# Distances from f32r high and low parts, and a schedule with one query or key projection per slot

## The chip, the cores and the metric

The kernel runs on one core of one Trainium2 chip. The metric is the device time of one execution in microseconds (us), from the first to the last instruction and what lies around them. Matrix products run on TensorE (PE in the profile, its weight loads PEld), elementwise work on VectorE (DVE), ScalarE (ACT) and GpSimd (POOL); the transfers of this kernel are issued by the SyncE queue (SP).

## The reference, cut to what matters

Four layers follow each other on x of shape (8, 512, 128): a distance attention, a mixture of experts, a linear attention, a block with token selection. The change touches only the first:

```python
def _cdist(Q, K):
    q2 = jnp.sum(Q * Q, axis=-1)
    k2 = jnp.sum(K * K, axis=-1)
    qk = jnp.einsum('hbtd,hbsd->hbts', Q, K)
    d2 = q2[..., :, None] + k2[..., None, :] - 2.0 * qk
    return jnp.sqrt(jnp.maximum(d2, 0.0))
P = X @ W_in + b_in                       # 16 heads, each 64 of Q, K, V, G
Q, K, V, G = jnp.split(P, splits, axis=-1)
W = jnp.power(EPS + _cdist(Q, K), -P_POW) # EPS 1e-4, P_POW 2
W = W / (EPS + jnp.sum(W, axis=-1, keepdims=True))
A = jnp.einsum('hbts,hbse->hbte', W, V)
H = G * A
return H @ W_out + b_out                  # heads side by side again
```

## The kernel before, in words

`build_attention` computes the first layer, `build_rest` the other three; the second begins when the first has ended. Each engine has its own instruction list, in a fixed order written out by hand, and the engines meet in semaphores.

The attention goes over 8 batches of 512 tokens. A batch has 16 heads, taken four at a time (a quad): 32 periods `j`, four to a batch (`q = j % 4`). Two heads (a pair, `r` = 0 or 1) lie one above the other in the 128 partitions, 64 rows each, so a product over 64 rows is issued once for each half `v`. Each period has four slots `k`. In slot `k` of period `j`, in this order, TensorE does (lines 401 to 427):

- `distances(j, k)`: two chunks `i` of 128 keys against 512 queries for the two heads, into the four banks of `sc`. Per chunk and half, two f32r products of the matrix `quarter` (0.25) with the high and the low part of the squared queries (L356), then one f32 product key by query (L361; the query is stored times -2). A wait on `s_d2` lets a slot begin once VectorE has emptied `sc`.
- projections for period `j + 1`: slot 0 Q0 and K0, slot 1 Q1 and K1, slot 2 G0, slot 3 G1. Each is three f32r products of split operands (`product`, L57) into a bank of `pj`.
- slot 0 `sums(j-2)` (column sums of the weights that POOL has added, L382), slot 1 `output(j-3)` (L390), slot 2 `weighted_values(j-1, 0)` (L374) and `key_norms(j+1)` (16 records of L342), slot 3 `weighted_values(j-1, 1)`; once per batch eight `values` products (four in slot 3 of q = 0, four in slot 1 of q = 1) and transposes in slot 2 of q = 2.

`pj` has three banks, used in rotation by everything but the distances and `weighted_values`. The list `bank_uses` numbers the uses; use number n waits until VectorE has emptied use n-3 (`bank`, line 306):

```python
n = use[name]
if n >= 3:
    pe.wait_ge(s_pj_free, n - 2)
return n % 3
```

VectorE goes through the same slots in the same order: four operations that add the key norms, cut at 0 and write `w` (L495), one operation for each projection (L472, L474, L478), then the gate times the values (L502), the sums (L507), the reciprocals (L511) and so on; in slot 0 of q = 2 `norm_apply` (L624, L627) for the next batch. ScalarE takes root, logarithm and exponential of `w` (L584, L588, L598). POOL has per period: `normalize(j-3)` (L287), `squares(j+1, 0)` and `squares(j+1, 1)` (L260, L264, L268, L270 each), then `add_chunks(j-1, u)` for u = 0 to 3, three adds each (L278, L281). `normalize` waits for the broadcast reciprocals, which go by way of four transfers of the SP queue from the sums of slot 0 and the reciprocals of slot 2 of the period before. `query` and `key` have three places each, so POOL may read them late.

Of the kernel before, what the change touches and what calls it, by code (L numbers as in the profile page):

```python
# [20 lines left out]
P = 128  # L21
# [39 lines left out]
def build_attention(nc, a, x1, dsum, drec):  # L61
# [3 lines left out]
    with ExitStack() as ctx:  # L65
# [15 lines left out]
        xn = sb("xn", [P, NC, D])  # L81
# [11 lines left out]
        quarter = sb("quarter", [P, P], F32R)  # L93
        ones = sb("ones", [P, 32])

        query = sb("query", [P, 3, T])
        key = sb("key", [P, 3, T])
        sqq = sb("sqq", [P, T])
        sqk = sb("sqk", [P, 2, T])
        sqs = [sb("sq_h", [P, 3, T], F32R), sb("sq_l", [P, 3, T], F32R)]  # L100
        k2 = sb("k2", [P, 2, 2, NC, 2])
        gT = sb("gT", [P, PAIRS, T])
# [30 lines left out]
        s_pj_free = sem("s_pj_free")  # L133
        s_sq = sem("s_sq")
# [24 lines left out]
        def bank_uses(j, k):  # L159
            names = []  # L160
            b, q = divmod(j, QUADS)
            if j + 1 < NQ:
                names += [("p", j + 1, i) for i in (((Q0, K0), (Q1, K1), (G0,), (G1,))[k])]
            if k == 0 and 0 <= j - 2 < NQ:
                names.append(("sum", j - 2))
            if k == 1 and q == 1 and b < B:
                names += [("v", b, n) for n in range(4, 8)]
            if k == 1 and 0 <= j - 3 < NQ:
                names.append(("out", j - 3))
            if k == 2 and j + 1 < NQ:  # L170
                names.append(("k2", j + 1))
# [26 lines left out]
        def _(sp):  # L198
# [19 lines left out]
            sp.wait_ge(s_xn, NC)  # L218
# [20 lines left out]
            for j in range(NQ):  # L239
# [5 lines left out]
                if q == 1 and b + 2 < B:  # L245
                    sp.wait_ge(s_xn, NC * (b + 2))
                    load_x(xa, b + 2, s_xa)
# [3 lines left out]
        def _(pool):  # L251
            nc.gpsimd.memset(ones[:, :], 1.0).then_inc(s_ones, 1)
            nc.gpsimd.memset(quarter[:, :].bitcast(F32), 0.25).then_inc(s_ones, 1)

            def squares(j, r):
# [4 lines left out]
                nc.gpsimd.tensor_tensor(sqq[:, :], query[:, g % 3, :], query[:, g % 3, :], ALU.mult).then_inc(s_sq, 1)  # L260
                pool.wait_ge(s_pj_free, use["p", j, 3 * r + 1] + 1)
                if j >= 1:
                    pool.wait_ge(s_pj, use["k2", j - 1] + 1)
                nc.gpsimd.tensor_tensor(sqk[:, r, :], key[:, g % 3, :], key[:, g % 3, :], ALU.mult).then_inc(s_sq, 1)  # L264
# [18 lines left out]
            def normalize(j):  # L283
# [4 lines left out]
                                        gT[:, 2 * q:2 * q + 2, :], ALU.mult).then_inc(s_hT, 1)  # L288

            for j in PERIODS:  # L290
                if 0 <= j - 3 < NQ:
                    normalize(j - 3)
                if j + 1 < NQ:
                    squares(j + 1, 0)
                    squares(j + 1, 1)
# [9 lines left out]
        def _(pe):  # L305
# [6 lines left out]
            def turn(b):  # L312
                pe.wait_ge(s_xn, NC * (b + 1))
                for h in range(2):
                    n = bank(("turn", b, h))
                    for c in range(2 * h, 2 * h + 2):
                        m = nc.tensor.transpose(pj[:, n, c % 2 * P:(c % 2 + 1) * P], xn[:, c, :], ident[:, :])
# [83 lines left out]
            def step(j, k):  # L401
# [3 lines left out]
                if j + 1 < NQ:  # L405
                    for i in ((Q0, K0), (Q1, K1), (G0,), (G1,))[k]:
                        projection(j + 1, i)
                if k == 0 and 0 <= j - 2 < NQ:
                    sums(j - 2)
# [921 lines left out]
```

## Time and profile before

| | before |
|---|---|
| runs, us | 1567.01, 1563.69, 1568.65 (median 1567.01) |
| profiled execution, us | 1569.49 |
| its span, us | 1567.7 |
| PE busy | 1466.7 (94%) |
| DVE busy | 977.1 (62%) |
| ACT busy | 1039.0 (66%) |
| POOL busy | 817.1 (52%) |
| granted TensorE clock, mean | 0.967 |
| attention, us from the span's start | 0 to about 1031 |

A busy time is the sum of an engine's instructions; matmul ends are modelled, so spacing of starts tells more than a duration. A granted clock of 1 is 2.4 GHz, of 0.5 it is 1.2 GHz. POOL has all its work in the attention.

### The profile page before, as it was taken

Reading aid. Unit: us, or ns where it says so; the run is one execution under the profiler, and the core shown is the slowest. Engines: PE = TensorE matmul, PEld = TensorE weight load, DVE = VectorE, ACT = ScalarE, POOL = GpSimd, SP = SyncE. Lnnn points to the kernel's source line nnn. Section 1 sums busy time; section 2 is a strip of 40 time slices with the busy share of each in tenths; the row PEclk is TensorE's granted clock in tenths of the full one; section 3 lists DMA queues with packets and bytes.
Section 4 is the critical chain, followed back from the end, with each engine's and each line's share of the span. In section 5 each row is a group of like instructions: output and inputs, shape, how many; then the busy total and the mean of one; then the engine's idle time right before and its main releaser. Section 6 shows DMA issues by size and latency. Waiting matters only on the chain. (4 is left out here: it accounts for less than half of the span.)

```text
span 1567.7 us, 18478 instructions
## 1 busy us (share of the span) xinstructions
PE 1466.7 (94%) x6704; PEld 811.4 (52%) x6704; DVE 977.1 (62%) x2082; ACT 1039.0 (66%) x834; POOL 817.1 (52%) x681
## 2 busy tenths in 40 slices
PE   6999999999999999999999999559999999999984
PEld 4544544554544544545545444135666666666653
DVE  4766676666666766776676665134375675665664
ACT  1789779869968977977977878424454554554531
POOL 5678878878879879879879878500000000000000
PEclk9999999999999999999999999769999999999995
DMA  3000010011001002001101101161110110110100
GB/s 106 1 15 22 15 42 22 14 36 28 15 15 48 15 15 49 15 15 38 25 15 28 28 15 40 30 196 59 54 61 1 61 61 1 62 55 7 61 5 10
DMA packets 45851, 54.96 MB, mean 35 GB/s; under 512 B 13824, under 2 KB 32640, under 8 KB 44608
## 3 DMA queue, kind: packets, MB, share of 16 engines
q1 hardware_dynamic: 45760, 53.77, 11.4%
q8 instruction: 54, 0.88, 0.2%
q14 instruction: 37, 0.30, 0.1%
HBM read 48.91 MB, written 4.85 MB: 34 GB/s over the span
## 5 line engine op out<-in xcount | busy, mean ns | idle before, releaser
L495 DVE TENSOR_SCALAR w<-sc,k 128x512 f32<-128x512 f32 x512 | 348.9, 743 | 148.2 <-PE sc L361 121.3
L584 ACT ACTIVATE w<-w 128x2048 f32<-128x2048 f32 x128 | 237.5, 1904 | 193.6 <-DVE w L495 193.2
L281 POOL TENSOR_TENSOR wsum<-wsum,w 128x512 f32<-128x512 f32 x256 | 327.1, 1278 | 20.1
L846 ACT ACTIVATE hr<-z,b 128x512 f32<-128x512 f32 x256 | 175.6, 686 | 226.4 <-PE z L57 226.3
L993 PE MATMUL y<-hr,w 128*128 128x512 f32 x512 | 261.4, 593 | 2.4 <-DVE yT L1199 2.4
L361 PE MATMUL sc<-query,key 64*128 64x512 f32 x1024 | 243.7, 594 | 0.0
L374 PE MATMUL av<-w,vt 128*64 128x512 f32 x1024 | 236.1, 603 | 6.7 <-ACT w L598 5.8
L588 ACT ACTIVATE w<-w 128x2048 f32<-128x2048 f32 x128 | 240.3, 1901 | 0.4
L598 ACT ACTIVATE w<-w 128x2048 f32<-128x2048 f32 x128 | 239.6, 1896 | 0.0
L57 PE MATMUL z<-xs_h,w_h 128*128 128x512 f32 x256 | 202.1, 789 | 0.1
L278 POOL TENSOR_TENSOR wsum<-w 128x512 f32<-128x512 f32 x128 | 163.5, 1277 | 8.8 <-ACT w L598 8.8
L260 POOL TENSOR_TENSOR sqq<-query 128x512 f32<-128x512 f32 x64 | 66.6, 1041 | 154.4 <-DVE query L472 154.2
L374 PEld LDWEIGHTS av<-w,vt 128*64 128x64 f32 x1024 | 68.6, 138 | 143.8 <-issue 136.0
L361 PEld LDWEIGHTS sc<-query,key 64*128 64x128 f32 x1024 | 99.7, 188 | 72.4 <-issue 61.4
L356 PE MATMUL sc<-sq_h,quarter 64*128 64x512 f32 x512 | 115.8, 447 | 12.6 <-DVE w L495 12.6
L502 DVE TENSOR_TENSOR gT<-av,gT 128x512 f32<-128x512 f32 x64 | 44.2, 691 | 131.3 <-PE av L374 131.3
L356 PE MATMUL sc<-sq_l,quarter 64*128 64x512 f32 x512 | 102.2, 393 | 0.0
L57 PE MATMUL z<-xs_l,w_h 128*128 128x512 f32 x256 | 101.4, 396 | 0.0
L993 PEld LDWEIGHTS y<-hr,w 128*128 128x128 f32 x512 | 90.7, 189 | 19.8 <-DVE yT L1199 2.8
L57 PE MATMUL z<-xs_h,w_l 128*128 128x512 f32 x256 | 100.9, 394 | 0.0
L1199 DVE SCALAR_TENSOR_TENSOR ye<-y,b,rb 128x512 f32<-128x512 f32 x56 | 41.9, 749 | 90.5 <-PE y L993 90.3
L356 PEld LDWEIGHTS sc<-sq_h,quarter 64*128 64x128 f32 x512 | 48.9, 185 | 92.0 <-issue 79.8
(154 smaller groups left out, 2166.6 us busy)
## 6 DMA issues: line engine op xcount, KB each, us to landing
hT<-head_recips SPq DMA_DIRECT2D x64, 256.0 KB, 4.0
rb<-routing SPq DMA_DIRECT2D x8, 2048.0 KB, 7.1
w<-in_W SPq DMA_DIRECT2D x16, 256.0 KB, 6.2
xa<-in_X SPq DMA_DIRECT2D x8, 256.0 KB, 4.5
xc<-in_X SPq DMA_DIRECT2D x8, 256.0 KB, 2.8
x<-xc SPq DMA_DIRECT2D x8, 256.0 KB, 4.1
out<-prod SPq DMA_DIRECT2D x8, 256.0 KB, 2.3
x<-x SPq DMA_DIRECT2D x1, 1792.0 KB, 10.2
```

The lines of the kernel that those rows point to most:

```text
L57: m = nc.tensor.matmul(out, lhsT[u], rhs[v], start=start and i == 0, stop=stop and i == 2)
L278: nc.gpsimd.tensor_tensor(wsum[:, u, :], w[:, j % 2, u, 0, :], w[:, j % 2, u, 1, :], ALU.add).then_inc(s_added, 1)
L281: nc.gpsimd.tensor_tensor(wsum[:, u, :], wsum[:, u, :], w[:, j % 2, u, c, :], ALU.add).then_inc(s_added, 1)
L356: nc.tensor.matmul(sc[:, i, v, :], quarter[halves[v], :], sqs[part][halves[v], g % 3, :], start=(part == 0), stop=False)
L361: m = nc.tensor.matmul(sc[:, i, v, :], key[halves[v], g % 3, c * P:(c + 1) * P], query[halves[v], g % 3, :], start=False, stop=True)
L374: m = nc.tensor.matmul(av[64 * v:64 * v + 64, :], vt[:, c, (2 * g + v) * E0:(2 * g + v + 1) * E0], w[:, j % 2, 2 * r + v, c, :], start=(c ...
L495: nc.vector.tensor_scalar(w[:, s, 2 * r + v, c, :], sc[:, i, v, :], k2[:, s, r, c, v:v + 1], 0.0, ALU.add, ALU.max).then_inc(s_d2, 1)
L584: nc.scalar.activation(w[:, slot, u, :, :], w[:, slot, u, :, :], ACT.Sqrt).then_inc(s_sqrt, 1)
L588: nc.scalar.activation(w[:, slot, u, :, :], w[:, slot, u, :, :], ACT.Ln, bias=ATT_EPS).then_inc(s_ln, 1)
L598: nc.scalar.activation(w[:, slot, u, :, :], w[:, slot, u, :, :], ACT.Exp, scale=-2.0).then_inc(s_w, 1)
L846: nc.scalar.activation(hr[:, n % 8, :], z[:, n % 2, :], ACT.Relu, bias=b1[:, n % NU:n % NU + 1]).then_inc(S["hr"], 1)
L993: m = nc.tensor.matmul(y[:, g % 2, :], w2[:, k, :], hr[:, n % 8, :], start=(i == 0), stop=(i == NF - 1))
```

## The change

The f32 product of key and query is replaced by three f32r products of high and low parts: key high by query high, key high by query low, key low by query high, each in the two row halves (per slot 12 instructions of one pass, where there were 4 of two passes). For that VectorE makes three operations of each query and key projection: the whole value (for POOL's squares), the high part in f32r, and, after a wait on the new semaphore `s_high`, the difference as the low part; the bank is handed back by the third. `query` and `key` have one place now, so the write of the whole value waits on `s_sq` until POOL has squared the one before. Signs and factors change (`quarter` 0.25 becomes `half` -0.5, the query is no longer times -2, VectorE subtracts and takes the minimum, the root has scale -2.0), with the same number of operations.

The order changes on TensorE and VectorE alike: slots 0 to 3 have Q0, K0, Q1, K1 of period `j + 1`; the gates G0 and G1 of period `j - 1` come in slots 0 and 1 (one period before they are used up, `gT` has two places in place of eight pairs). The key norms of the second pair are made in slot 1 of the next period, those of the first in slot 2, 8 records each. In slot 1 `output` stands ahead of `values`. POOL squares the second pair at the start of its own period, after `normalize`, then the first pair of the next. The normalized input is written over `xa` (`xn` is gone), and the SP queue loads the next `xa` after the transposes in place of after the normalization. The `step` functions of both engines (lines 401 and 527) follow `bank_uses` below.

```diff
@@ -90,16 +89,18 @@
         nsel = sb("nsel", [P, 2, P])
-        quarter = sb("quarter", [P, P], F32R)
+        half = sb("half", [P, P], F32R)
         ones = sb("ones", [P, 32])
...
-        query = sb("query", [P, 3, T])
-        key = sb("key", [P, 3, T])
+        query = sb("query", [P, T])
+        key = sb("key", [P, T])
+        queries = [sb("query_h", [P, 3, T], F32R), sb("query_l", [P, 3, T], F32R)]
+        keys = [sb("key_h", [P, 3, T], F32R), sb("key_l", [P, 3, T], F32R)]
         sqq = sb("sqq", [P, T])
-        sqk = sb("sqk", [P, 2, T])
+        sqk = sb("sqk", [P, T])
         sqs = [sb("sq_h", [P, 3, T], F32R), sb("sq_l", [P, 3, T], F32R)]
         k2 = sb("k2", [P, 2, 2, NC, 2])
-        gT = sb("gT", [P, PAIRS, T])
+        gT = sb("gT", [P, 2, 2, T])
         hT = sb("hT", [P, 2, 2, T])
...
@@ -160,15 +162,19 @@
             if j + 1 < NQ:
-                names += [("p", j + 1, i) for i in (((Q0, K0), (Q1, K1), (G0,), (G1,))[k])]
+                names.append(("p", j + 1, (Q0, K0, Q1, K1)[k]))
+            if k < 2 and 0 <= j - 1 < NQ:
+                names.append(("p", j - 1, (G0, G1)[k]))
             if k == 0 and 0 <= j - 2 < NQ:
                 names.append(("sum", j - 2))
+            if k == 1 and 0 <= j < NQ:
+                names.append(("k2", j, 1))
+            if k == 1 and 0 <= j - 3 < NQ:
+                names.append(("out", j - 3))
             if k == 1 and q == 1 and b < B:
                 names += [("v", b, n) for n in range(4, 8)]
-            if k == 1 and 0 <= j - 3 < NQ:
-                names.append(("out", j - 3))
             if k == 2 and j + 1 < NQ:
-                names.append(("k2", j + 1))
+                names.append(("k2", j + 1, 0))
             if k == 2 and q == 2 and b >= 1:
...
@@ -243,25 +249,25 @@
                 if q == 1 and b + 2 < B:
-                    sp.wait_ge(s_xn, NC * (b + 2))
+                    sp.wait_ge(s_pj, use["turn", b + 1, 1] + 1)
                     load_x(xa, b + 2, s_xa)
...
             nc.gpsimd.memset(ones[:, :], 1.0).then_inc(s_ones, 1)
-            nc.gpsimd.memset(quarter[:, :].bitcast(F32), 0.25).then_inc(s_ones, 1)
+            nc.gpsimd.memset(half[:, :].bitcast(F32), -0.5).then_inc(s_ones, 1)
...
                     pool.wait_ge(s_sq, 4 * g)
-                nc.gpsimd.tensor_tensor(sqq[:, :], query[:, g % 3, :], query[:, g % 3, :], ALU.mult).then_inc(s_sq, 1)
+                nc.gpsimd.tensor_tensor(sqq[:, :], query[:, :], query[:, :], ALU.mult).then_inc(s_sq, 1)
                 pool.wait_ge(s_pj_free, use["p", j, 3 * r + 1] + 1)
-                if j >= 1:
-                    pool.wait_ge(s_pj, use["k2", j - 1] + 1)
-                nc.gpsimd.tensor_tensor(sqk[:, r, :], key[:, g % 3, :], key[:, g % 3, :], ALU.mult).then_inc(s_sq, 1)
+                if g >= 1:
+                    pool.wait_ge(s_pj, use["k2", *divmod(g - 1, 2)] + 1)
+                nc.gpsimd.tensor_tensor(sqk[:, :], key[:, :], key[:, :], ALU.mult).then_inc(s_sq, 1)
                 pool.wait_ge(s_sq, 4 * g + 1)
...
@@ -285,14 +291,15 @@
                 nc.gpsimd.tensor_tensor(hT[:, j % 2, :, :], hT[:, j % 2, :, :],
-                                        gT[:, 2 * q:2 * q + 2, :], ALU.mult).then_inc(s_hT, 1)
+                                        gT[:, j % 2, :, :], ALU.mult).then_inc(s_hT, 1)
...
                     normalize(j - 3)
+                if 0 <= j < NQ:
+                    squares(j, 1)
                 if j + 1 < NQ:
                     squares(j + 1, 0)
-                    squares(j + 1, 1)
                 if j == -1:
...
@@ -333,14 +340,12 @@
-            def key_norms(j):
-                n = bank(("k2", j))
-                pe.wait_ge(s_sq, 8 * j + 6)
-                for r in range(2):
-                    for c in range(NC):
-                        i = 2 * (NC * r + c)
-                        m = nc.tensor.matmul(pj[:, n, i:i + 2], sqk[:, r, c * P:(c + 1) * P], nsel[:, 0, 0:64:32],
-                                             start=(i == 0), stop=True, skip_group_check=True)
+            def key_norms(j, r):
+                n = bank(("k2", j, r))
+                pe.wait_ge(s_sq, 8 * j + 4 * r + 2)
+                for c in range(NC):
+                    m = nc.tensor.matmul(pj[:, n, 2 * c:2 * c + 2], sqk[:, c * P:(c + 1) * P], nsel[:, 0, 0:64:32],
+                                         start=(c == 0), stop=True, skip_group_check=True)
                 m.then_inc(s_pj, 1)
...
@@ -351,15 +356,15 @@
                 for i in range(2):
+                    c = 2 * k % NC + i
                     for part in range(2):
                         for v in range(2):
-                            nc.tensor.matmul(sc[:, i, v, :], quarter[halves[v], :], sqs[part][halves[v], g % 3, :],
+                            nc.tensor.matmul(sc[:, i, v, :], half[halves[v], :], sqs[part][halves[v], g % 3, :],
                                              start=(part == 0), stop=False)
-                for i in range(2):
-                    c = 2 * k % NC + i
-                    for v in range(2):
-                        m = nc.tensor.matmul(sc[:, i, v, :], key[halves[v], g % 3, c * P:(c + 1) * P],
-                                             query[halves[v], g % 3, :], start=False, stop=True)
+                    for part, (x, y) in enumerate(((0, 0), (0, 1), (1, 0))):
+                        for v in range(2):
+                            m = nc.tensor.matmul(sc[:, i, v, :], keys[x][halves[v], g % 3, c * P:(c + 1) * P],
+                                                 queries[y][halves[v], g % 3, :], start=False, stop=(part == 2))
                     m.then_inc(s_sc, 1)
...
@@ -464,28 +470,33 @@
             def projection(j, i):
-                q = j % QUADS
                 r, part = divmod(i, 3)
-                s = (2 * j + r) % 3
-                source, bias = pj[:, bank(("p", j, i)), :], bqkg[:, 2 * q + r, part:part + 1]
-                if part == 0:
-                    nc.vector.tensor_scalar(query[:, s, :], source, bias, -2.0, ALU.add, ALU.mult).then_inc(s_pj_free, 1)
-                elif part == 1:
-                    nc.vector.tensor_scalar(key[:, s, :], source, bias, None, ALU.add).then_inc(s_pj_free, 1)
-                else:
-                    if j >= QUADS:
-                        dve.wait_ge(s_hT, j - QUADS + 1)
-                    nc.vector.tensor_scalar(gT[:, 2 * q + r, :], source, bias, None, ALU.add).then_inc(s_pj_free, 1)
-
-            def key_norms(j):
-                nc.vector.tensor_copy(k2[:, j % 2, :, :, :].rearrange("p r c v -> p (r c v)"),
-                                      pj[:, bank(("k2", j)), 0:4 * NC]).then_inc(s_pj_free, 1)
+                g = 2 * j + r
+                n = bank(("p", j, i))
+                source, bias = pj[:, n, :], bqkg[:, 2 * (j % QUADS) + r, part:part + 1]
+                if part == 2:
+                    if j >= 2:
+                        dve.wait_ge(s_hT, j - 1)
+                    nc.vector.tensor_scalar(gT[:, j % 2, r, :], source, bias, None, ALU.add).then_inc(s_pj_free, 1)
+                    return
+                whole, (high, low) = (query, queries) if part == 0 else (key, keys)
+                if g >= 1:
+                    dve.wait_ge(s_sq, 4 * (g - 1) + part + 1)
+                nc.vector.tensor_scalar(whole[:, :], source, bias, None, ALU.add)
+                nc.vector.tensor_scalar(high[:, g % 3, :], source, bias, None, ALU.add).then_inc(s_high, 1)
+                dve.wait_ge(s_high, 2 * g + part + 1)
+                nc.vector.scalar_tensor_tensor(low[:, g % 3, :], source, bias, high[:, g % 3, :].bitcast(F32),
+                                               ALU.add, ALU.subtract).then_inc(s_pj_free, 1)
+
+            def key_norms(j, r):
+                nc.vector.tensor_scalar(k2[:, j % 2, r, :, :].rearrange("p c v -> p (c v)"),
+                                        pj[:, bank(("k2", j, r)), 0:2 * NC], 0.5, None, ALU.mult).then_inc(s_pj_free, 1)
...
                 s, r = j % 2, k // 2
-                if k == 0:
-                    dve.wait_ge(s_pj_free, use["k2", j] + 1)
+                if k % 2 == 0:
+                    dve.wait_ge(s_pj_free, use["k2", j, r] + 1)
                 if j >= 2:
...
@@ -493,13 +504,12 @@
                         nc.vector.tensor_scalar(w[:, s, 2 * r + v, c, :], sc[:, i, v, :], k2[:, s, r, c, v:v + 1], 0.0,
-                                                ALU.add, ALU.max).then_inc(s_d2, 1)
+                                                ALU.subtract, ALU.min).then_inc(s_d2, 1)
...
             def weighted_values(j, r):
-                g = 2 * (j % QUADS) + r
                 dve.wait_ge(s_av, 2 * j + r + 1)
                 dve.wait_ge(s_pj_free, use["p", j, 3 * r + 2] + 1)
-                nc.vector.tensor_tensor(gT[:, g, :], av[:, :], gT[:, g, :], ALU.mult).then_inc(s_gated, 1)
+                nc.vector.tensor_tensor(gT[:, j % 2, r, :], av[:, :], gT[:, j % 2, r, :], ALU.mult).then_inc(s_gated, 1)
...
@@ -581,7 +592,7 @@
                     act.wait_ge(s_d2, 16 * j + 2 * (4 * r + 3) + v + 1)
-                    nc.scalar.activation(w[:, slot, u, :, :], w[:, slot, u, :, :], ACT.Sqrt).then_inc(s_sqrt, 1)
+                    nc.scalar.activation(w[:, slot, u, :, :], w[:, slot, u, :, :], ACT.Sqrt, scale=-2.0).then_inc(s_sqrt, 1)
...
                     act.wait_ge(s_sqrt, j * 4 + u + 1)
```

## Rows read from the trace of the kernel before

**Rows 1.** Page: busy us of each engine, share of the span, instructions.

```profile
PE 1466.7 (94%) x6704; PEld 811.4 (52%) x6704; DVE 977.1 (62%) x2082; ACT 1039.0 (66%) x834; POOL 817.1 (52%) x681
```

**Rows 2.** Timeline, PE, one period: start us, length, engine, line, out<-in, count, [idle].

```profile
503.44 0.50 PE L356 MATMUL sc<-sq_h,quarter 64*128 64x512 f32 x2
...
508.87 0.50 PE L356 MATMUL sc<-sq_h,quarter 64*128 64x512 f32 x2
...
515.01 0.50 PE L356 MATMUL sc<-sq_h,quarter 64*128 64x512 f32 x2
...
522.32 1.95 PE L342 MATMUL pj<-nsel,sqk 128*128 128x2 f32 x16
...
524.19 0.50 PE L356 MATMUL sc<-sq_h,quarter 64*128 64x512 f32 x2
...
525.23 1.88 PE L361 MATMUL sc<-query,key 64*128 64x512 f32 x8
...
527.04 0.50 PE L57 MATMUL pj<-xh,wqkg_h 128*128 128x512 f32 x1
...
527.61 0.40 PE L57 MATMUL pj<-xl,wqkg_h 128*128 128x512 f32 x1
...
527.93 3.65 PE L374 MATMUL av<-w,vt 128*64 128x512 f32 x16
...
531.52 0.50 PE L57 MATMUL pj<-wv_h,xh 128*128 128x512 f32 x1
```

**Rows 3.** Timeline, DVE: the copy of the key norms, four periods apart.

```profile
403.37 0.17 DVE L481 COPY k<-pj 128x16 f32<-128x16 f32 x1 [1.17 <-PE pj L342]
...
524.30 0.17 DVE L481 COPY k<-pj 128x16 f32<-128x16 f32 x1 [1.17 <-PE pj L342]
```

**Rows 4.** Timeline, DVE, slot 0 and the start of slot 1 of one period.

```profile
505.66 2.73 DVE L495 TENSOR_SCALAR w<-sc,k 128x512 f32<-128x512 f32 x4 [1.42 <-PE sc L361]
...
508.30 0.74 DVE L472 TENSOR_SCALAR query<-pj,bqkg 128x512 f32<-128x512 f32 x1
...
509.62 0.68 DVE L507 TENSOR_SCALAR srow<-pj 128x512 f32<-128x512 f32 x1
```

**Rows 5.** Timeline, DVE: a cast and the subtraction that waits for it (experts' weights).

```profile
1037.04 0.43 DVE L1186 CAST w_h<-w 128x512 fp32r<-128x512 f32 x1
...
1037.50 0.69 DVE L1188 TENSOR_TENSOR w_l<-w,w_h 128x512 fp32r<-128x512 f32 x1
```

**Rows 6.** Page, costliest groups: out<-in xcount | busy us, mean ns | idle before, releaser.

```profile
L1199 DVE SCALAR_TENSOR_TENSOR ye<-y,b,rb 128x512 f32<-128x512 f32 x56 | 41.9, 749 | 90.5 <-PE y L993 90.3
```

**Rows 7.** Timeline, PE: a use of pj that waited for its bank.

```profile
424.59 0.50 PE L57 MATMUL pj<-wv_h,xh 128*128 128x512 f32 x1 [0.45 <-DVE query L472]
```

**Rows 8.** Timeline, POOL: squares, the first of twelve adds, and the next normalize.

```profile
579.44 1.04 POOL L260 TENSOR_TENSOR sqq<-query 128x512 f32<-128x512 f32 x1 [3.71 <-DVE query L472]
580.44 1.04 POOL L264 TENSOR_TENSOR sqk<-key 128x512 f32<-128x512 f32 x1
...
583.36 1.28 POOL L278 TENSOR_TENSOR wsum<-w 128x512 f32<-128x512 f32 x1
...
599.14 2.41 POOL L287 TENSOR_TENSOR hT<-hT,gT 128x1024 f32<-128x1024 f32 x1
```

**Rows 9.** Timeline, DVE: `norm_apply` with POOL idle, and with POOL at work.

```profile
5.42 1.11 DVE L627 TENSOR_SCALAR xn<-xa,mv,rstd 128x128 f32<-128x128 f32 x4
...
573.06 3.01 DVE L627 TENSOR_SCALAR xn<-xa,mv,rstd 128x128 f32<-128x128 f32 x4
```

**Rows 10.** Who waited for whom, 60 to 1130 us: total us, times, longest.

```profile
POOL hT L287 <- DMA hT<-head_recips: 16.2, 9, 11.2
```

**Rows 11.** Timeline, PE: work after idle stretches, at full and at half clock.

```profile
21.70 3.54 PE L342 MATMUL pj<-nsel,sqk 128*128 128x2 f32 x16 [2.82 <-POOL sqk L264]
...
92.17 0.50 PE L356 MATMUL sc<-sq_h,quarter 64*128 64x512 f32 x2 [2.83 <-DVE w L495]
...
1008.98 3.75 PE L390 MATMUL pj<-hT,wout 128*128 128x512 f32 x4 [2.47 <-POOL hT L287]
```

More of the change, by code:

```diff
@@ L80, in build_attention @@
         holder = sb("holder", [P, 1])
-        xn = sb("xn", [P, NC, D])
         xs = [sb("xh", [P, 2, T], F32R), sb("xl", [P, 2, T], F32R)]
@@ L133, in build_attention @@
         s_pj_free = sem("s_pj_free")
+        s_high = sem("s_high")
         s_sq = sem("s_sq")
@@ L217, in _ @@
             load_x(xc, 0, s_xc)
-            sp.wait_ge(s_xn, NC)
+            sp.wait_ge(s_pj, use["turn", 0, 1] + 1)
             load_x(xa, 1, s_xa)
@@ L316, in turn @@
                     for c in range(2 * h, 2 * h + 2):
-                        m = nc.tensor.transpose(pj[:, n, c % 2 * P:(c % 2 + 1) * P], xn[:, c, :], ident[:, :])
+                        m = nc.tensor.transpose(pj[:, n, c % 2 * P:(c % 2 + 1) * P], xa[:, c, :], ident[:, :])
                     m.then_inc(s_pj, 1)
@@ L405, in step @@
                 if j + 1 < NQ:
-                    for i in ((Q0, K0), (Q1, K1), (G0,), (G1,))[k]:
-                        projection(j + 1, i)
+                    projection(j + 1, (Q0, K0, Q1, K1)[k])
+                if k < 2 and 0 <= j - 1 < NQ:
+                    projection(j - 1, (G0, G1)[k])
                 if k == 0 and 0 <= j - 2 < NQ:
                     sums(j - 2)
+                if k == 1 and 0 <= j < NQ:
+                    key_norms(j, 1)
+                if k == 1 and 0 <= j - 3 < NQ:
+                    output(j - 3)
                 if k == 1 and q == 1 and b < B:
@@ L412, in step @@
                         values(b, n)
-                if k == 1 and 0 <= j - 3 < NQ:
-                    output(j - 3)
-                if k == 2 and 0 <= j - 1 < NQ:
-                    weighted_values(j - 1, 0)
+                if k >= 2 and 0 <= j - 1 < NQ:
+                    weighted_values(j - 1, k - 2)
                 if k == 2 and j + 1 < NQ:
-                    key_norms(j + 1)
+                    key_norms(j + 1, 0)
                 if k == 2 and q == 2 and b >= 1:
@@ L422, in step @@
                     turn(b + 1)
-                if k == 3 and 0 <= j - 1 < NQ:
-                    weighted_values(j - 1, 1)
                 if k == 3 and q == 0 and b < B:
@@ L449, in norm_apply @@
             def norm_apply(b):
-                layernorm_apply(nc, dve, xa, 0, xn, mv, std[:, :], rstd[:, :], b, s_std, s_rstd, s_xn)
+                layernorm_apply(nc, dve, xa, 0, xa, mv, std[:, :], rstd[:, :], b, s_std, s_rstd, s_xn)
             def turned(b):
@@ L531, in step @@
                 if j + 1 < NQ:
-                    for i in ((Q0, K0), (Q1, K1), (G0,), (G1,))[k]:
-                        projection(j + 1, i)
+                    projection(j + 1, (Q0, K0, Q1, K1)[k])
+                if k < 2 and 0 <= j - 1 < NQ:
+                    projection(j - 1, (G0, G1)[k])
                 if k == 0 and 0 <= j - 2 < NQ:
@@ L537, in step @@
                     norm_apply(b + 1)
+                if k == 1 and 0 <= j < NQ:
+                    key_norms(j, 1)
+                if k == 1 and 0 <= j - 3 < NQ:
+                    output(j - 3)
                 if k == 1 and q == 1 and b < B:
@@ L542, in step @@
                         norm_stats(b + 1)
-                if k == 1 and 0 <= j - 3 < NQ:
-                    output(j - 3)
-                if k == 2 and 0 <= j - 1 < NQ:
-                    weighted_values(j - 1, 0)
+                if k >= 2 and 0 <= j - 1 < NQ:
+                    weighted_values(j - 1, k - 2)
                 if k == 2 and j + 1 < NQ:
-                    key_norms(j + 1)
+                    key_norms(j + 1, 0)
                 if k == 2 and q == 2 and b >= 1:
@@ L554, in step @@
                     turned(b + 1)
-                if k == 3 and 0 <= j - 1 < NQ:
-                    weighted_values(j - 1, 1)
                 if k == 3 and q == 0 and b < B:
```

## Prediction, made before the changed kernel was run

> **What bounds the kernel now.** I read the busy shares first: PE is busy 94% of the span, no other engine over 66% [rows 1]. Next the timeline of TensorE over one period in the steady stretch. Its starts follow each other without a hole: distances of slot 0 at 503.44, of slot 1 at 508.87, of slot 2 at 515.01, of slot 3 at 524.19, and the last work of the plain period ends where the values begin, at 531.52 [rows 2]. So the slots last 5.43, 6.14, 9.18 and 7.33 us, a plain period 28.08, and TensorE's own work sets it. Four periods (a batch, with eight value products and a normalization) last 524.30 - 403.37 = 120.93 us [rows 3], 30.2 on the average.
>
> **What TensorE saves.** In slot 3 the four f32r pairs of the squares take 525.23 - 524.19 = 1.04 us (0.34 to the second, then 0.23 each; the halves of a pair run beside each other). The key-query products are eight records, 527.04 - 525.23 = 1.81 us. Then three products of 0.23 and a transition: 527.93 - 527.04 = 0.89 [rows 2]. After the change the slot has 2 x 2 + 2 x 3 = 10 f32r pairs and the three products in one run: 0.34 + 11 x 0.23 + 0.32 = 3.20 us to the weighted values, where there were 3.74. That is 0.54 a slot; the new pairs have the form of the squares' pairs (64 rows, 64x512), so I take their spacing. The key norms move 8 of their 16 records from slot 2 to slot 1: (524.19 - 522.32) / 2 = 0.93 us [rows 2]. The projections are two, two, one, one per slot as before. New slots: 4.89, 6.53, 7.71, 6.79; sum 25.92, a saving of 2.16 a period and 69 us in 32, if TensorE stays the bound.
>
> **What VectorE gets.** Spacing in rows: four distance operations 508.30 - 505.66 = 2.64, one projection (509.62 - 508.30) / 2 = 0.66 [rows 4]. A projection of a query or key becomes three. The whole value costs 0.66. The high part ends before the low part may start: 0.74 and a hop; a cast and the subtraction that waits for it start 0.46 apart with 0.43 busy [rows 5], so 0.78. The low part is a three-operand operation, 0.75 by the experts' own [rows 6] (0.69 as a plain subtraction [rows 5]), 0.67 to the next start. Sum 2.11, or 2.19 until the bank is free, in place of 0.66 or 0.74. Four a period: 5.8 us more. VectorE stays under 90%, which would be hidden; what counts is where it lies.
>
> **The bank.** With the new order the uses of `pj` in slot 1 are K0, G1, key norms, output; `output` is three uses behind K0 and waits for its low part. (Before, it came three behind the sums.) The rows show such a wait once a batch: a value product three uses behind Q1 waited 0.45 us for the query operation [rows 7]. Count from the start of TensorE's slot 0. The first chunk of distances is ready after five pairs, 1.5 us. VectorE then runs without a hole: distances 2.64, Q0 2.11, G0 0.66, sums 0.60, distances of slot 1 2.64, K0 2.19: bank free at 12.35. TensorE would be at `output` at 4.89 + 0.34 + 15 x 0.23 + 0.1 + 0.93 = 9.7. It waits 2.7 us there. From there output 1.85 (its share of slot 1, with the hop), slot 2 7.71, slot 3 6.79: the plain period is **28.7**, 0.6 longer than before, although TensorE works 2.2 less.
>
> **POOL's loop.** `query` has one place, so VectorE's Q0 of the next period waits until POOL has squared Q1 of the one before, and POOL does that only after twelve adds and `normalize`. Who is queued behind: on VectorE everything of slot 0 after the distances, then the distances of slot 1 and K0; on POOL the adds wait behind the squares of K0. That closes a ring. POOL, from K0 handed over: hop 0.08, square of the key to the first add 583.36 - 580.44 = 2.92, the adds 599.14 - 583.36 = 15.78, `normalize` 2.35, square of Q1 1.04 [rows 8], hop 0.05: 22.2. VectorE, from the start of Q0 to K0 handed over: 2.11 + 0.66 + 0.60 + 2.64 + 2.19 = 8.2. Ring: **30.4 us**. It is longer than the bank's 28.7, so it sets plain periods. In the trace of before POOL never stood in a ring: it waited 3.71 for the query here [rows 8].
>
> **Sum over a batch.** q = 0: four value products in slot 3 (12 x 0.23 + 0.2 = 3.0) lie in the bank's path, not in POOL's: 28.7 + 3.0 = 31.7. q = 1: four value products after output, the same 31.7. q = 2: `norm_apply` lies between sums and the distances of slot 1, in both paths. It takes 3.01 beside POOL's work and 1.11 where POOL is idle [rows 9]; at its new place POOL has only the end of one square left and then waits for K0, so I take 1.6 (bounds 1.3 and 3.2): 32.0. q = 3: 30.4. Sum 125.8, against 120.93: +4.9 a batch, +34 us over periods 3 to 31. The first three periods lack `output` and part of POOL's list: -2. The last has no projections to make and only saves: -2. The start-up gains and loses (POOL's splitting of weights now stands ahead of the second squares; VectorE's operations are longer): taken at 0, bounds -4 and +4. Layers two to four (from 1031 us) are untouched. The order of the SP queue costs nothing: the transposes it now waits for lie in q = 2, and the queue gets to that wait only after the reciprocals of q = 3. The DMA of the reciprocals is a third path to `normalize`; it kept POOL waiting 16.2 us in all, 11.2 of it at the end of the attention, so about 5 in the rest [rows 10], and POOL now comes later. Total +30 to +31. Against the profiled execution's 1569.5 that is 1600; its own time lies 2.5 over the median, so against the median 1598.
>
> **The rivals.**
> The clock falls in the new wait (chance 0.20). The wait at `output` is 2.7 us in q = 0 and 1 up to some 4 in q = 2, and the 2-column key norms lie ahead of it. In the rows one idle stretch of 2.82 was followed by key norms in 3.54 us (1.95 elsewhere [rows 2]), so at 1.2 GHz; another of 2.83 was followed by work at 2.4 GHz; after 2.47 with little work ahead `output` took 3.75 for 1.88 [rows 11]. If it falls in most periods, about 5 us of work at half rate lose 2.6 each, and TensorE's path is the longer one: 31.3, 34.3 twice, 33.9, in a batch 133.8, +12.9, +90 in all less 4: 1653.
> The Trainium skill, page "TensorE: Matmul & The Clock Gate", section "Why this matters for your kernels", warns that idle gaps between bursts of matmuls bring the array back to half rate; by that rule this rival would be the rule in q = 2 and a matter of luck elsewhere.
> Only the bank (0.13): POOL's ring turns out shorter than 28.7, by shorter adds or an earlier start. Then 31.7, 31.7, 31.3, 28.7: +2.5 a batch, 1567 + 17 - 4 = 1580.
> TensorE stays the bound (0.12), the other side: the wait for K0 is hidden, because VectorE catches up or the f32r operations write faster than an f32 one (a cast of the same size takes 0.43 [rows 5]). With 2.2 saved a period and nothing given back: 1567 - 69 = 1498. It decides as soon as K0's bank is free 9.7 us into the period; VectorE's work ahead of that would have to shrink by 2.7 of 12.3 us, and POOL's ring by as much again, so it is not likely.
> The halves of the new pairs don't run beside each other (0.05): 6 x 0.23 = 1.4 more per slot, 3.5 in the bank's path: 28.7 becomes 32.2, a batch 137.4, 1567 + 115 - 4 = 1678. Against it: the squares' pairs do run so [rows 2].
>
> **How the numbers follow.** Forecast (bank and POOL's ring together, clock up) 0.50, time 1598. With a slow `norm_apply` it would be 11 higher (1.6 a batch of seven); a ring 0.5 us off moves two periods of four, 7 us; a clock that falls now and then adds 10 to 25. The range leaves out the two outer cases (0.12 and 0.05) and takes in the others: 1575 to 1658. This kernel's runs can tell about 0.3% (5 us). Faster: 0.12 and a rest of the start-up bounds, 0.13. Same: 0.04, the low tail of the bank case. Slower: 0.83.
>
> **What would show it.** Right: on TensorE f32r pairs 0.23 apart through the whole slot; idle time before `output` (L390), released by VectorE's key operation; idle time of VectorE before the query's first operation in slot 0, released by POOL's square; a batch of about 126 us, with plain periods of 30.4; PE's busy time 60 to 70 us lower and its share under 90%; POOL almost without a wait. A granted clock well under 1 between 100 and 950 us would show the clock's case. Wrong: a period under 28 us, `output` without a wait, or f32r operations of VectorE under 0.6 us.

## The result

| | before | after |
|---|---|---|
| median of the runs, us | 1566.6 | 1652.2 (1649.8 to 1653.9) |
| ratio | | 1.0547, 95% interval 1.0523 to 1.0571 |
| profiled execution's span, us | 1567.7 | 1648.9 |
| attention ends at, us from the start | 1031 | 1114 |

The change costs 86 us. Layers two to four are untouched: of the span's 81 us, 82 lie ahead of the first instruction of `build_rest` (1031.4 before, 1113.5 after), so all of it is in the attention.

The page of the changed kernel, the lines that answer to [rows 1]; the third is the group of `output` (line 390 before, 395 now; columns as in [rows 6]):

```profile
PE 1477.6 (90%) x7216; PEld 883.9 (54%) x7216; DVE 1146.0 (70%) x2370; ACT 1039.1 (63%) x834; POOL 819.9 (50%) x681
PEclk9999999999999998999999999977999999999995
...
L395 PE MATMUL pj<-hT,wout 128*128 128x512 f32 x128 | 103.2, 952 | 91.2 <-DVE key_l L488 77.3
```

`output` now has 77.3 us of idle time ahead of it, ended by VectorE's low part of the key, and its records last 952 ns in the mean, where 592 is their mean in the kernel before between 60 and 960 us. TensorE has less work and is busy longer (1477.6 us for 1466.7): part of the work runs at half rate.

Slot 0 and slot 1 of one period (q = 2) of the changed kernel, TensorE and VectorE, and POOL where it waits:

```profile
609.19 2.42 POOL L293 TENSOR_TENSOR hT<-hT,gT 128x1024 f32<-128x1024 f32 x1 [4.00 <-DMA hT<-head_recips]
...
611.82 1.07 PE L387 MATMUL pj<-wsum,ones 128*32 128x512 f32 x8
612.71 0.75 DVE L485 TENSOR_SCALAR query<-pj,bqkg 128x512 f32<-128x512 f32 x1 [0.71 <-POOL sqq L266]
612.81 0.50 PE L362 MATMUL sc<-sq_h,half 64*128 64x512 f32 x2
...
616.28 1.28 DVE L638 TENSOR_SCALAR xa<-xa,mv,rstd 128x128 f32<-128x128 f32 x4
...
616.83 0.95 PE L347 MATMUL pj<-nsel,sqk 128*128 128x2 f32 x8
617.49 2.71 DVE L506 TENSOR_SCALAR w<-sc,k 128x512 f32<-128x512 f32 x4
620.12 0.73 DVE L485 TENSOR_SCALAR key<-pj,bqkg 128x512 f32<-128x512 f32 x1
620.78 0.73 DVE L486 TENSOR_SCALAR key_h<-pj,bqkg 128x512 fp32r<-128x512 f32 x1
621.55 0.75 DVE L488 SCALAR_TENSOR_TENSOR key_l<-pj,bqkg,key_h 128x512 fp32r<-128x512 f32 x1
622.35 3.78 PE L395 MATMUL pj<-hT,wout 128*128 128x512 f32 x4 [4.58 <-DVE key_l L488]
622.38 1.04 POOL L270 TENSOR_TENSOR sqk<-key 128x512 f32<-128x512 f32 x1 [5.67 <-DVE key_l L488]
626.07 0.79 PE L362 MATMUL sc<-sq_h,half 64*128 64x512 f32 x2
```

`output` of the kernel before, at full clock:

```profile
513.20 1.88 PE L390 MATMUL pj<-hT,wout 128*128 128x512 f32 x4
```

In the changed kernel TensorE has done its list of slot 1 up to `output` at 617.8, VectorE comes to K0 at 620.12 and hands its bank back at 622.3, and `output` starts 0.05 us later, at half clock (3.78 us for 1.88). The granted clock is 1.00 from 590.0 to 617.8 us, 0.50 from 622.3 to 627.0 and 0.99 from there to 640.0. The normalization takes 1.28 where it took 3.01 [rows 9]. The reciprocals come once a period, in slot 2 (VectorE, changed kernel):

```profile
533.25 0.24 DVE L521 RECIPROCAL srec<-ssum 128x16 f32<-128x16 f32 x1
...
564.15 0.24 DVE L521 RECIPROCAL srec<-ssum 128x16 f32<-128x16 f32 x1
...
600.88 0.24 DVE L521 RECIPROCAL srec<-ssum 128x16 f32<-128x16 f32 x1
...
635.78 0.24 DVE L521 RECIPROCAL srec<-ssum 128x16 f32<-128x16 f32 x1
...
666.55 0.24 DVE L521 RECIPROCAL srec<-ssum 128x16 f32<-128x16 f32 x1
```

A batch is 666.55 - 533.25 = 133.3 us, where it was 120.9 [rows 3] and the forecast's sum was 125.8; the period up to 564.15 takes 30.9. Who waited for whom in the attention of the changed kernel (total us, times, longest):

```profile
PE pj L395 <- DVE key_l L488: 77.3, 28, 4.6
...
POOL hT L293 <- DMA hT<-head_recips: 43.9, 20, 10.8
...
DVE query L485 <- POOL sqq L266: 8.3, 5, 4.2
```

The wait for K0's bank is there in all 28 full periods, 2.8 us in the mean. VectorE waited for POOL's square five times in all: the ring that the forecast took as the longer path is not what sets most periods of this kernel.

### The profile page after: what moved, and what is told of

The parts are those of the page before. It is cut to its first block and busy times, and to the rows that moved or that the text cites. A ratio compares the mean times of both kernels' runs of the same rounds, so it can differ in the third digit from the quotient of the medians.

```text
span 1648.9 us, 19955 instructions
## 1 busy us (share of the span) xinstructions
PE 1477.6 (90%) x7216; PEld 883.9 (54%) x7216; DVE 1146.0 (70%) x2370; ACT 1039.1 (63%) x834; POOL 819.9 (50%) x681
## 5 line engine op out<-in xcount | busy, mean ns | idle before, releaser
L506 DVE TENSOR_SCALAR w<-sc,k 128x512 f32<-128x512 f32 x512 | 348.4, 742 | 80.4 <-PE sc L366 80.4
L395 PE MATMUL pj<-hT,wout 128*128 128x512 f32 x128 | 103.2, 952 | 91.2 <-DVE key_l L488 77.3
L270 POOL TENSOR_TENSOR sqk<-key 128x512 f32<-128x512 f32 x64 | 66.7, 1042 | 158.7 <-DVE key_l L488 155.7
L362 PE MATMUL sc<-sq_h,half 64*128 64x512 f32 x512 | 121.0, 468 | 4.0 <-DVE w L506 4.0
L362 PE MATMUL sc<-sq_l,half 64*128 64x512 f32 x512 | 105.7, 408 | 0.0
L366 PE MATMUL sc<-query_h,key_h 64*128 64x512 f32 x512 | 104.9, 403 | 0.0
L366 PE MATMUL sc<-query_l,key_h 64*128 64x512 f32 x512 | 104.5, 401 | 0.0
L366 PE MATMUL sc<-query_h,key_l 64*128 64x512 f32 x512 | 104.0, 399 | 0.0
L362 PEld LDWEIGHTS sc<-sq_h,half 64*128 64x128 f32 x512 | 51.3, 195 | 93.4 <-issue 41.7
```

What stands on the lines that cost most here:

```text
L362: nc.tensor.matmul(sc[:, i, v, :], half[halves[v], :], sqs[part][halves[v], g % 3, :], start=(part == 0), stop=False)
L366: m = nc.tensor.matmul(sc[:, i, v, :], keys[x][halves[v], g % 3, c * P:(c + 1) * P], queries[y][halves[v], g % 3, :], start=False, stop=(p ...
L506: nc.vector.tensor_scalar(w[:, s, 2 * r + v, c, :], sc[:, i, v, :], k2[:, s, r, c, v:v + 1], 0.0, ALU.subtract, ALU.min).then_inc(s_d2, 1)
```

## The experiments

Theory A, that of the forecast: K0's bank and POOL's ring. Theory B, its first rival: the bank and the clock that falls in the wait. Rivals to both: the wait alone, TensorE's work, the order of the change as such. Each kernel was compared with the kernel before run on the same chip (1567.5 to 1569.6 in these).

### TensorE's part alone

In the kernel before, with `query` and `key` as f32r tiles; it leaves out the low parts and VectorE's operations for them, and all three products read the same two tiles:

```diff
                 for i in range(2):
+                    c = 2 * k % NC + i
...
-                for i in range(2):
-                    c = 2 * k % NC + i
-                    for v in range(2):
-                        m = nc.tensor.matmul(sc[:, i, v, :], key[halves[v], g % 3, c * P:(c + 1) * P],
-                                             query[halves[v], g % 3, :], start=False, stop=True)
+                    for part in range(3):
+                        for v in range(2):
+                            m = nc.tensor.matmul(sc[:, i, v, :], key[halves[v], g % 3, c * P:(c + 1) * P],
+                                                 query[halves[v], g % 3, :], start=False, stop=(part == 2))
```

> The kernel before, schedule and all, with query and key written once, as f32r, and the f32 product of key and query replaced by three f32r products of these same tiles (the low parts and VectorE's operations for them are left out). It measures what TensorE alone saves. By the spacing in the changed kernel's trace a slot takes 3.43 us to the weighted values where it took 3.74: 0.31 x 128 = 40 us, 1527. By the forecast's 0.54 a slot: 69 us, 1498.

Measured: 1529.0, ratio 0.9748 (0.9730 to 0.9766), 39.4 us faster: 0.31 a slot. The forecast's 0.54 is wrong, and one slot shows by what (TensorE, this kernel):

```profile
526.90 0.50 PE L357 MATMUL sc<-sq_h,quarter 64*128 64x512 f32 x2
...
528.63 0.88 PE L361 MATMUL sc<-query,key 64*128 64x512 f32 x6
529.43 0.50 PE L57 MATMUL pj<-xh,wqkg_h 128*128 128x512 f32 x1
...
530.33 1.94 PE L374 MATMUL av<-w,vt 128*64 128x512 f32 x8
```

The pairs go at 0.23 behind the first step of 0.34, but from the last of them (528.63 + 2 x 0.23 = 529.09) to the first product over all 128 rows it is 0.34, and 0.34 again to the second (at 529.77). I had run pairs and products into one row at 0.23. The slot takes 3.43 us, not 3.20.

### One operation of VectorE in place of three

In the changed kernel, leaving out the whole value and the low part (POOL and the three products then read the f32r part):

```diff
...
-                nc.vector.tensor_scalar(whole[:, :], source, bias, None, ALU.add)
-                nc.vector.tensor_scalar(high[:, g % 3, :], source, bias, None, ALU.add).then_inc(s_high, 1)
-                dve.wait_ge(s_high, 2 * g + part + 1)
-                nc.vector.scalar_tensor_tensor(low[:, g % 3, :], source, bias, high[:, g % 3, :].bitcast(F32),
-                                               ALU.add, ALU.subtract).then_inc(s_pj_free, 1)
+                nc.vector.tensor_scalar(high[:, g % 3, :], source, bias, None, ALU.add).then_inc(s_pj_free, 1)
```

> The changed kernel, schedule and all, with one operation of VectorE for each query and key projection (the f32r part alone; the whole value and the low part are left out, POOL squares the f32r part, the three products read it three times). TensorE's work and order, the banks and POOL's list are those of the changed kernel. Theory: K0's bank is free 2.9 us earlier, 9.5 us into the period, before TensorE comes to output; no wait, no fall of the clock, 26.8 to 27.5 a plain period, a batch of 115 to 118, 1520 to 1540. Rival: the order itself (gates later, key norms in two parts, POOL's squares late) costs the time, over 1600.

Measured: 1530.8, ratio 0.9756 (0.9740 to 0.9773), about the time of the kernel with TensorE's part alone. So the new order costs next to nothing on balance, and what stands between 1531 and 1652 is VectorE's two more operations per projection, which VectorE has room for (70% busy in the changed kernel). One thing was not as expected: `output` still waited for K0's bank in 15 periods, mostly 0.4 to 1.4 us.

### The clock kept up

In the changed kernel, ahead of `output` in slot 1:

```diff
+            def fill(j):
+                q = j % QUADS
+                pe.wait_ge(s_gated, 2 * (j - 1))
+                for _ in range(15 if q == 2 else 10):
+                    nc.tensor.matmul(av[:, :], half[:, :], xs[0][:, (j // QUADS) % 2, :], start=True, stop=True)
...
+                if k == 1 and 3 <= j < NQ - 1:
+                    fill(j)
```

> The changed kernel with extra f32r products of 128x512 into av, ten (fifteen in q = 2) right ahead of output in slot 1 of periods 3 to 30, so that TensorE works through most of its wait for K0's bank (2.35 us, 3.6 to 4.6 in q = 2). Nothing else changes; the extra products are overwritten. Theory (the fallen clock costs the rest): output takes 1.9 us in place of 3.0 to 3.8, the granted clock between 100 and 1000 us is over 0.98, a batch falls from 133 to about 127 us (plain path 29.2, POOL's ring 30.4), the kernel from 1652 to about 1609, although it does 300 more products. Rival (the wait itself and what lies behind it cost the time, the clock only follows): 1652 or slower.

Measured: 1610.1, ratio 1.0272 (1.0252 to 1.0291). Busy time in 60 to 960 us (columns: stretch, us, busy of PE, PEld, DVE, ACT, POOL with counts, PEclk, DMA share, GB/s), first the changed kernel, then this one, and `output` in this one:

```profile
60.00:960.00 900.00, 822.52 (x4491) 469.45 (x4492) 701.91 (x1194) 668.03 (x389) 688.73 (x572) 0.94 0.09 22
```

```profile
60.00:960.00 900.00, 885.91 (x4991) 523.98 (x4989) 734.01 (x1242) 695.12 (x404) 719.10 (x597) 1.00 0.09 23
```

```profile
632.20 1.98 PE L395 MATMUL pj<-hT,wout 128*128 128x512 f32 x4 [0.20 <-DVE key_l L496]
```

TensorE has 315 more products to do and the kernel is 42 us faster: the clock is 1.00 for 0.94, `output` takes 1.98 for 3.78, and in all 28 periods it still starts 0.05 to 0.06 us after K0's bank is free. A batch is 126.8. So the fallen clock, theory B, accounts for 42 us. With the clock up VectorE does wait for POOL in two periods of each batch, 0.2 us in one and 1.1 us in the other, as here:

```profile
654.54 0.75 DVE L493 TENSOR_SCALAR query<-pj,bqkg 128x512 f32<-128x512 f32 x1 [1.12 <-POOL sqq L266]
```

### The bank taken out of the way

In the changed kernel, in the numbering, on TensorE and on VectorE alike:

```diff
+                if k == 1 and 0 <= j - 3 < NQ:
+                    output(j - 3)
                 if j + 1 < NQ:
                     projection(j + 1, (Q0, K0, Q1, K1)[k])
...
-                if k == 1 and 0 <= j - 3 < NQ:
-                    output(j - 3)
```

> The changed kernel with output(j-3) ahead of K0 in slot 1, on TensorE, VectorE and in the numbering of the banks: output then lies three uses behind Q0, not behind K0. Bank theory with POOL's ring: the wait at output is gone, the clock stays up, and the ring of 30.4 us plus 0.6 for VectorE's output operation, now inside it, sets the period: waits of VectorE's query operation for POOL's square in most periods, a batch of 125 us, 1597. Rival without a ring: TensorE's own 26.8 a plain period sets the pace, a batch of 116 us, 1530. Rival without the bank: no change, 1652.

Measured: 1605.9, ratio 1.0237 (1.0215 to 1.0260). The batch is 126.4, and now VectorE does wait for POOL (total, times, longest):

```profile
DVE query L485 <- POOL sqq L266: 41.4, 16, 4.2
```

So the ring is real, and it shows more the shorter the other path is. (`output` is now due Q0's bank, and it waits for that one 14 times, 20.8 us in all.) The next kernel takes `normalize` out of it:

```diff
-                if 0 <= j - 3 < NQ:
-                    normalize(j - 3)
                 if 0 <= j < NQ:
-                    squares(j, 1)
+                    squares(j, 1, (0,))
+                if 0 <= j - 3 < NQ:
+                    normalize(j - 3)
+                if 0 <= j < NQ:
+                    squares(j, 1, (1,))
```

> As the kernel with output ahead of K0, and POOL squares the query of the second pair ahead of normalize, the rest of its squares behind it. Ring theory: normalize (2.35 us) leaves the ring through the query, 30.4 + 0.6 - 2.3 = 28.7, and the one through the gates is 28.9: a batch of 118 to 119 us, about 50 us faster than the kernel with output ahead alone, some 1546. Rival: no ring, the same time as that kernel.

Measured: 1572.0, ratio 1.0016 (1.0003 to 1.0029): 34 us off, not 50 (its batches last 119.2 to 123.7 us where 118 to 119 were expected; why was not separated), and the wait falls to

```profile
DVE query L495 <- POOL sqq L272: 12.3, 11, 1.8
```

### The ring in the changed kernel

The same splitting of POOL's squares, and three of its adds in its wait for the key, in the changed kernel with nothing else altered:

```diff
                 if j + 1 < NQ:
-                    squares(j + 1, 0)
+                    squares(j + 1, 0, (0,))
+                if 0 <= j - 1 < NQ:
+                    add_chunks(j - 1, 0)
+                if j + 1 < NQ:
+                    squares(j + 1, 0, (1,))
...
-                    for u in range(4):
+                    for u in range(1, 4):
```

> The changed kernel, its order of TensorE and VectorE untouched, with POOL's list alone reordered: query square of the second pair ahead of normalize, the first head's adds between the squares of Q0 and K0. POOL's ring is then 24 us and binds nowhere; the wait at output for K0's bank stays. If the bank and the fallen clock alone set the time of the changed kernel: 1640 to 1652. If POOL's ring carries part of it (the forecast had it as the longer path): under 1620.

Measured: 1660.0, ratio 1.0573 (1.0518 to 1.0628), not faster. The total alone doesn't decide, because the adds slow something else down: the normalization in q = 2 takes 4.03 us for 1.28, and `output` behind it waits 6.50, where the changed kernel has 3.5 to 4.6:

```profile
625.82 4.03 DVE L652 TENSOR_SCALAR xa<-xa,mv,rstd 128x128 f32<-128x128 f32 x4
...
634.64 3.53 PE L409 MATMUL pj<-hT,wout 128*128 128x512 f32 x4 [6.50 <-DVE key_l L502]
```

The plain periods do decide. The second one of a batch takes 30.9 to 31.0 us, where the changed kernel has 30.8 to 31.0 in all but one batch, although VectorE never waits for POOL any more. So the ring carries next to nothing in the changed kernel. With the extra products as well, to see whether it does so once the clock is up:

> The changed kernel with the extra products ahead of output (clock up) and POOL's list reordered as in the kernel with the add between alone (its ring 24 us). Theory: with the clock up the bank's path is 29.2 us a plain period and POOL's ring of 30.4 is the longer one, so taking the ring away gives back 1 us or so in plain periods, less a slower normalization in q = 2 beside the adds (up to 3 us a batch): between 1595 and 1615. Rival: the ring never carries anything; then only the slower normalization is seen, 1615 to 1625.

Measured: 1626.3, ratio 1.0364 (1.0349 to 1.0379), 16 slower than with the extra products alone. The time is that of the rival, but the trace says otherwise. Here are the reciprocals that bound the two plain periods of a batch, first in the kernel with the extra products alone, then in this one:

```profile
612.73 0.24 DVE L529 RECIPROCAL srec<-ssum 128x16 f32<-128x16 f32 x1
...
642.30 0.24 DVE L529 RECIPROCAL srec<-ssum 128x16 f32<-128x16 f32 x1
...
672.89 0.24 DVE L529 RECIPROCAL srec<-ssum 128x16 f32<-128x16 f32 x1
```

```profile
626.68 0.25 DVE L543 RECIPROCAL srec<-ssum 128x16 f32<-128x16 f32 x1
...
655.98 0.24 DVE L543 RECIPROCAL srec<-ssum 128x16 f32<-128x16 f32 x1
...
685.33 0.24 DVE L543 RECIPROCAL srec<-ssum 128x16 f32<-128x16 f32 x1
```

The two plain periods of the batch take 29.57 and 30.59 with the ring, 29.30 and 29.35 without it. So with the clock up the ring does set one plain period in each batch, 1.2 us longer, as theory A had it. What makes the total 16 us longer all the same lies in q = 2 (VectorE, this kernel):

```profile
605.08 4.08 DVE L660 TENSOR_SCALAR xa<-xa,mv,rstd 128x128 f32<-128x128 f32 x4
```

The normalization takes 4.08 us beside POOL's adds for 1.12 in the kernel with the extra products alone, 3.0 more in the path to K0, and the wait of 3 us that this leaves ahead of `output` brings the clock down there (2.7 to 3.8 us for `output`). The period into q = 2 takes 36.1 us for 31.6.

### Towards a faster kernel

Both reorderings together (output first, adds in between):

> As the kernel with output ahead and the query's square early, and POOL makes the three adds of the first head (3.9 us) between the square of Q0 and the square of K0, where it waits 3 to 6 us for the key. If POOL's ring still sets the period there, it loses 3.9 us and falls under TensorE's own work (26.8 a plain period): a batch of about 115 to 117 us in place of 122.5, about 1525 to 1535, faster than the kernel before. Rival: VectorE's chain and the short waits of TensorE at the key norms set the pace, no change, 1572.

Measured: 1578.6, ratio 1.0064 (1.0041 to 1.0087), 7 slower than without the adds in between. The plain periods did fall to 26.9, TensorE's own work, but in q = 2 the same thing happens as above:

```profile
579.59 4.73 DVE L652 TENSOR_SCALAR xa<-xa,mv,rstd 128x128 f32<-128x128 f32 x4
...
587.60 1.79 PE L361 MATMUL pj<-nsel,sqk 128*128 128x2 f32 x8 [4.75 <-DVE oT L543]
```

TensorE waits 4.75 us at the key norms, and these run at half clock (1.79 for 0.95). Moving the gates one slot later did not help:

> As the kernel with the add between, and the gates G0 and G1 one slot later on TensorE and VectorE (slots 1 and 2), so that VectorE reaches K0 0.66 us earlier. If VectorE's chain from Q0 to K0 is what TensorE still waits for, 0.66 us a period, some 20 us faster than that kernel; if TensorE's own work is the bound, no change.

Measured: 1582.1, ratio 1.0086 (1.0061 to 1.0111). Moving the normalization behind K0 did:

```diff
-                if k == 0 and q == 2 and b + 1 < B:
-                    norm_apply(b + 1)
                 if k == 1 and 0 <= j < NQ:
                     key_norms(j, 1)
+                if k == 1 and q == 2 and b + 1 < B:
+                    norm_apply(b + 1)
```

> As the kernel with the add between the squares, and VectorE applies the normalization for the next batch (4.7 us there, beside POOL's adds) at the end of slot 1 of q = 2 in place of the end of slot 0, so behind K0 and not ahead of it. In the trace of the kernel with the add between, plain periods take 26.9 us and the one from q = 1 to q = 2 takes 33.6 to 35.8, with TensorE idle 4.75 us at the key norms and its clock down behind that. If it is VectorE's chain in q = 2 that costs this, the period falls to about 28, a batch from 122.9 to 116, the kernel to about 1530, faster than the kernel before. Rival: the time moves to slot 2, where the distances wait for VectorE, no change, 1579.

Measured: 1554.1, ratio 0.9905 (0.9888 to 0.9921). This kernel, with the products of the change, is 15 us faster than the one before and 98 faster than the change as made. Its batch is 119.4, not the 116 expected (1530 for the kernel): in q = 2 `turn` waits 1.8 us for VectorE and the work behind that runs at half clock. VectorE is busy 788 us of the 900 between 60 and 960. The last kernel was slower again:

> As that, and the statistics for the next batch (1.1 us on VectorE) in slot 3 of q = 1 in place of slot 1, where VectorE also has four value additions. If VectorE's backlog in slot 1 of q = 1 is what makes the value periods 2 us longer than TensorE's own work, about 1 us a batch, 1522; else the same.

Measured: 1563.9, ratio 0.9963 (0.9941 to 0.9986), 10 slower. In its trace the period with the eight value products takes 35.5 us for 33.9 in three of seven batches, with a granted clock of 0.97 for 0.98 between 60 and 960 us; why was not followed.

## Why the prediction was right or wrong

The sign, the place and the mechanism of the main wait were right; the size was wrong: 1598 forecast, 1652 measured. The first rival, the clock that falls in the wait (chance 0.20), is what happened, and its price of 1653 is close in part by luck: it put the half clock at 2.6 us a period, where a plain period takes 31.0 with it and 29.3 without, 1.7 (both lengths stand in the trace of the changed kernel and in that of the one with POOL's list reordered); and it had the bank's path at full clock 0.6 too short (28.7 for 29.3). The two nearly cancel.

- VectorE's projection: right. Its three operations start 0.66 and 0.77 apart and last 0.75. K0's bank was forecast free 12.35 us after the start of slot 0; in the period that starts at 573.94 it is free at 586.33, 12.39.
- The wait at `output`: right. 2.7 and up to 4 forecast, 2.34 to 4.58 measured (1.99 once, at the start).
- What TensorE saves: mis-sized, 0.54 a slot for 0.31. The term is the passage from half-row pairs to full-row products (0.34 for the 0.23 taken), twice in the row read as one run. On the bank's path lie two such slots a period, 0.46 of the 0.6 us by which its plain period at full clock is longer than forecast.
- POOL's ring, "it sets plain periods": wrong in the changed kernel. With the clock down the bank's path takes 31.0 in a plain period, not 28.7, and the ring of 30.4 hides behind that; taking it out left the period as it was. Its length was right: with the clock up it sets one plain period of each batch, 30.6 for 29.35. The sum had it set two periods of four, 1.7 us each; measured at full clock it is about 1.5 us a batch.
- The clock: this is the step that failed. The sum let TensorE go on at full clock behind the wait at `output` and put nothing in for the half rate. The rows had it both ways after 2.8 us of idle time [rows 11], I gave it 0.20, and in the changed kernel `output` ran at full clock throughout in only 3 of 28 periods. With the clock held up the kernel takes 1610: 42 of the 54 us by which the forecast missed. Of the other 12, about 7 lie in the batch, 126.8 at full clock for the forecast's 125.8, and the slot's term lies in that; the remaining 5 or so lie outside the steady batches, where the forecast took 4 off for the ends, and were not followed.
- The Trainium skill, page "TensorE: Matmul & The Clock Gate", section "Why this matters for your kernels", warns that idle gaps between bursts of matmuls bring the array back to half rate. The trace agrees: 0.94 with the gaps, 1.00 with the gaps filled. The clock fell behind all seven gaps of q = 2, and, where the prediction had read the rule as a matter of luck, behind 18 of the 21 others too.
- The normalization at its new place: right, 1.12 to 1.28 for the 1.6 taken. Given POOL's adds beside it, it takes 4.0 to 4.1.
- The DMA path of the reciprocals: POOL waited 43.9 us for it, 10.8 of them at the end of the attention, so 33 where about 5 was forecast. Mostly nobody waited for POOL behind that, but in three periods VectorE did, 0.7 to 1.4 us each; the q = 2 shown above is one (4.00 of POOL at 609.19, then 0.71 of VectorE), and its wait at `output` is 4.58 where the other periods of its kind have about 3.6.
- The signs: the pairs 0.23 apart and the wait at `output` came. PE's busy time rose by 11 us where 60 to 70 less was forecast, because part of it ran at half clock, and POOL, forecast almost without a wait, waited 150.8 us for the key.

The account in batches: 120.9 before; with TensorE's saving and without VectorE's part it is 3 to 5 less (115.5 to 118.4 in the two kernels near 1530). VectorE's two operations bring it to 126.8 at full clock, through K0's bank and for about 1.5 of it through POOL's ring, and the clock brings it to 133.0.

## What to carry to other kernels

An engine with 30% of idle time can still be the one that sets the pace: when a change makes the handing back of a rotating buffer later, walk the rotation and find who is due that buffer next. A wait of 2 to 4 us on TensorE, such as the ones here, is to be priced twice, once as the wait and once as the half rate of the work behind it, and if the rows don't decide whether the clock holds, filling the wait with products settles it. A path that is compared with another must be compared at the other's real length: a second ring shows only when the first is gone or has become shorter. And a reordering that is meant to take one path out can slow another one: read the period in which that path should show, not the total alone. Here the total said that the ring never counts, and the plain periods said that it does once the clock is up.

## What the runs showed of the hardware that was not expected

- The clock fell after idle stretches of 2.35 us with 0.95 us of 2-column products ahead of them, in most of the periods. What the work at half clock behind them cost was 1.7 us in a plain period.
- `norm_apply`, four operations of VectorE of 128x128 from SBUF to SBUF, takes 1.1 to 1.3 us with POOL idle for all or most of it, 3.0 beside its squares and their split [rows 9], and 4.0 to 4.7 beside its adds. VectorE's operations that read PSUM in the changed kernel keep their time: four of L506 take 2.69 to 2.73 us wherever they fall, beside the adds or not.
- f32r pairs of 64 rows follow each other at 0.23 us, but the passage to products over 128 rows takes 0.34, and so does the step behind the first of them.
